# Second half of Q with the blocks of x in other buffers, and the first scores ahead of V's first quarter

## The reference, cut to what matters

```
h = layernorm(x)
q = rope(h @ Wq)    32 heads of 128;  k = rope(ctx @ Wk), v = ctx @ Wv    8 heads of 128
w = softmax(where(mask, 30 * tanh(q.k * scale / 30), -1e30))
x = x + (w @ v) @ Wo
x = x + base(layernorm(x)) + lora(layernorm(x))     top-2 of 8 experts, rank 16
```

## Time and profile before

| | us |
|---|---|
| median of 3 runs (lowest, highest) | 2150.79 (2147.84, 2157.55) |
| profiled execution, its own time | 2149.18 |
| its span in the trace | 2147.4 |
| TensorE busy in the span | 2129.3 (99%) |
| DVE, ACT, POOL busy | 1663.9, 882.2, 292.8 |

### The profile page before, as it was taken

The page is one execution under the profiler, slowest core; times in us unless marked ns, Lnnn a source line. Parts: engine busy times, 40 slices in busy tenths (PEclk is TensorE's granted clock), DMA queues, the critical chain, the costliest instruction groups (busy, mean ns, idle before and its releaser), DMA issues.

```text
span 2147.4 us, 26381 instructions
## 1 busy us (share of the span) xinstructions
PE 2129.3 (99%) x9429; PEld 1727.0 (80%) x9429; DVE 1663.9 (77%) x2571; ACT 882.2 (41%) x1342; POOL 292.8 (14%) x359
## 2 busy tenths in 40 slices
PE   9999999999999999998999999999999999999999
PEld 7888888888888888876778777777787777888887
DVE  6966889888887666676878789997998889857443
ACT  3323243222241111155555566655665556423221
POOL 0340001111131000013111111111112111100000
PEclk9999999999999999999999999999999999999999
DMA  8698597655596655698766786689677965696741
GB/s 327 233 343 285 212 336 275 230 212 216 215 338 230 212 202 200 235 272 271 198 197 187 225 242 181 205 271 276 193 194 218 306 187 161 212 373 263 293 183 64
DMA packets 201715, 508.50 MB, mean 237 GB/s; under 512 B 20592, under 2 KB 45808, under 8 KB 199536
## 3 DMA queue, kind: packets, MB, share of 16 engines
q1 hardware_dynamic: 181104, 443.31, 62.7%
q0 software_dynamic: 20480, 63.50, 9.3%
HBM read 357.26 MB, written 149.16 MB: 236 GB/s over the span
## 4 chain that ended last, share of the span: by engine, by line
PE 86%; DMA 7%; DVE 4%; issue 1%; ACT 1%; POOL 0%; SPq 0%; ACTq 0%; DVEq 0%; POOLq 0%
PE ps L377 28%; PE ps L379 28%; PE ps L378 28%; DMA X2D<-stg 2%; DMA RB<-rD 2%; DMA rD<-r 1%; PE ps L914 1%; DVE Rl L330 1%; DVE Y L984 1%; DMA raw<-gran 1%; DVE ps L330 1%; DMA r<-rT 1%; DVE Pl L330 0%; DVE ps L899 0%; DVE Al L330 0%
## 5 line engine op out<-in xcount | busy, mean ns | idle before, releaser
L377 PE MATMUL ps<-Ah,Rh 128*128 128x512 f32 x1024 | 399.6, 390 | 2.6 <-DVE Y L984 2.6
L379 PE MATMUL ps<-Ah,Rl 128*128 128x512 f32 x1024 | 399.2, 390 | 0.0
L378 PE MATMUL ps<-Al,Rh 128*128 128x512 f32 x1024 | 399.0, 390 | 0.0
L378 PE MATMUL ps<-Xq,qW 128*128 128x512 f32 x896 | 348.5, 389 | 0.0
L377 PE MATMUL ps<-Xq,qW 128*128 128x512 f32 x896 | 348.5, 389 | 0.0
L379 PE MATMUL ps<-Xq,qW 128*128 128x512 f32 x896 | 348.5, 389 | 0.0
L330 DVE TENSOR_TENSOR Rl<-raw,Rh 128x1024 fp32r<-128x1024 f32 x174 | 212.3, 1220 | 57.1 <-ACT Rh L326 56.7
L326 ACT ACTIVATE Rh<-raw 128x1024 fp32r<-128x1024 f32 x176 | 185.4, 1055 | 148.5 <-PE ps L379 118.0
L377 PEld LDWEIGHTS ps<-Ah,Rh 128*128 128x128 f32 x1024 | 192.5, 188 | 45.0 <-DVE Y L984 3.0
L379 PEld LDWEIGHTS ps<-Ah,Rl 128*128 128x128 f32 x1024 | 192.5, 188 | 40.5
L378 PEld LDWEIGHTS ps<-Al,Rh 128*128 128x128 f32 x1024 | 192.5, 188 | 40.1
(11 more groups left out here) (217 smaller groups left out, 3869.1 us busy)
## 6 DMA issues: line engine op xcount, KB each, us to landing
raw<-gran SPq DMA_DIRECT2D x177, 512.0 KB, 6.1
QSD<-qW SPq DMA_DIRECT2D x64, 512.0 KB, 3.0
qD<-qt SPq DMA_DIRECT2D x128, 256.0 KB, 3.2
qW<-QSD SPq DMA_DIRECT2D x64, 512.0 KB, 3.7
qf<-qD SPq DMA_DIRECT2D x64, 512.0 KB, 8.3
RB<-rD POOLq DMA_DIRECT2D x128, 256.0 KB, 7.0
qraw<-gran SPq DMA_DIRECT2D x48, 512.0 KB, 4.3
kD<-kst SPq DMA_DIRECT2D x32, 512.0 KB, 3.8
```

The costliest lines, as they stand in the source:

```text
L377: put("pe", waits, lambda e: e.matmul(pe_out, lh, rh, start=first, stop=False, skip_group_check=more))
L378: put("pe", [], lambda e: e.matmul(pe_out, lh, rl, start=False, stop=False, skip_group_check=more))
L379: return put("pe", [], lambda e: e.matmul(pe_out, ll, rh, start=False, stop=last, skip_group_check=more), mark)
```

## The change

In the second half of Q the blocks of x lie in other buffers. Product i reads block i as before, but from buffer Xq[ORDER[cp][i]]: 3, 2, 4, 0, 1, 5, 6 for products 0 to 6. The loads of the second half are listed in that order too. `late_q`, which lets the filler's first raw loads start, is still the first product of quad 13. In the plan, the scores of group 0 stand at t = -16, -15, -14, -13, so that TensorE's order is S0, VQ1, S1, S2, VQ2, S3, VQ3 where it was VQ1, S0, S1, VQ2, S2, S3, VQ3 (S0 to S3 are the four scores of group 0). Nothing else is changed; the number of instructions and of bytes is the same.

```diff
+        ORDER = [range(7), (3, 2, 4, 0, 1, 5, 6)]
+
         def x_load(cp):
             got = []
-            for n in range(7):
-                d = [dma(f(Xq[n][:, 2 * k:2 * k + 2, 1, :]), XcD[cp, n, :, 2 * k:2 * k + 2],
-                         x_free[n] + Xc_store[cp, n], f"d_xq{n}{k}", 512) for k in range(2)]
+            for i, n in enumerate(ORDER[cp]):
+                d = [dma(f(Xq[n][:, 2 * k:2 * k + 2, 1, :]), XcD[cp, i, :, 2 * k:2 * k + 2],
+                         x_free[n] + Xc_store[cp, i], f"d_xq{n}{k}", 512) for k in range(2)]
...
             def product(i, dst, first, waits):
                 s, wm, kept = next(weights)
+                x = ORDER[cp][i]
...
-                    m = three(dst, lh, ll, Xq[i][:, k, 0, :], Xq[i][:, k, 1, :], first and k == 0, k == 3,
+                    m = three(dst, lh, ll, Xq[x][:, k, 0, :], Xq[x][:, k, 1, :], first and k == 0, k == 3,
...
-                x_free[i] = [m]
+                x_free[x] = [m]
...
-                    late_q = x_free[0]
+                    late_q = x_free[ORDER[1][0]]
...
-        first = {0: ((-15, -14, -13, -12), -11, -9, (-7, -6, -5, -4)),
+        first = {0: ((-16, -15, -14, -13), -11, -9, (-7, -6, -5, -4)),
```

## The result

| | before | after |
|---|---|---|
| median, us (20 runs of each) | 2157.64 | 2164.14 |
| lowest and highest, us | 2138.53, 2167.76 | 2156.34, 2172.57 |
| profiled execution, us (span) | 2149.18 (2147.4) | 2156.43 (2154.6) |
| last matmul of Q to first of the projection, us | 64.5 | 77.3 |
| last matmul of Q to the one of the projection that waits for Y, us | 78.1 | 90.4 |

The ratio of the times is 1.0042, with a 95% interval of 1.0024 to 1.0060. It is worked out from all forty runs and is not the ratio of the medians, which lie 6.5 us apart; the means lie 9.2 us apart. The change makes the kernel slower, by 9 us (5 to 13), less than the 0.5% that I called no change, though the interval reaches past it. The forecast was 1 us faster.

What follows compares the result with a forecast made beforehand. TensorE bounds the kernel, busy 2129.3 of 2147.4 us; only its waits and half clock can be won. Terms of -0.8, zeros and -0.2 made -1.0 us, from 2150.8 to 2149.8; range 2144.5 to 2157.

Steps and rivals of the forecast that it cites:

- Later context: Context splits and V's weight loads after Q come later: cost 0, other bound a 5.4 us stall and 1.4 us half clock.
- The end of Q on the queues: Last store of Q 2 to 4 us earlier, as 2 MB load ahead of the rush; up to 3.7 us, counted at nothing.
- S0 in front: At Q's end S0 starts without a wait ahead of VQ1 and covers the wait for bank l0: 0.8 us gained.
- The start of the second half: Xq[3] and Xq[4], needed earlier from 627.7 on, fit narrowly: cost 0, bounds 0 and 3 us.
- The sum: Whole kernel: -0.8 for l0, three zeros, -0.2 for relief of the blocked exponential; together -1.0 us.
- B: Rival: raw ring late in the first filler quarters, VQ2 waits, ACT and DVE stand behind it: +4 us, 2154.8; chance 0.22.
- A: Rival: after Q, last store lands before 957, V7 split in time, DMA chain ends earlier: -5.5 us, 2145.3; chance 0.18.
- C: Rival: the start of the second half stalls for Xq[3] or Xq[4]: +2 us, 2152.8; chance 0.11.
- D: Rival: all stalls between Q's end and the attention go: 2140.1 us; chance 0.02.

Runs made afterwards that it cites:

- e3: Kernel before, with only the first split of the context for V also waiting for product 4 of the last quad (8.2 us late): ratio 1.0075.
- e15: Kernel before with the context late as in e3, plus eight extra raw buffers for V1, V2, V3, ctx3 and V4 to V7: ratio 1.0003.
- e9: Changed kernel with eight raw buffers of their own for the loads of V1, V2, V3, ctx3 and V4 to V7: ratio 1.0032.
- e2: Kernel before with only the scores of group 0 at their new places, old order of the buffers: ratio 1.0033.
- e1: Kernel before with only the new ORDER of the buffers, scores at their old places: ratio 1.0081.
- e7: Kernel before with the raw loads of V0, V1 and V2 put ahead of all context parts: ratio 0.9999.

## Why the prediction was wrong

**The failed step is "Later context": priced at 0, it costs 16 us (11 to 21) when it comes alone.** I saw its mechanism. V1's load moves by 8 us, V4 to V7 and ctx3 hang on the same ring, and the prediction says so. Then I priced it only at TensorE's next user of that data: VQ2 needs V1 at 939.6. There it was right. V1 was issued at 931.15, 1.8 us later than I had it (3.2 counted from Q's end, which came 1.3 us earlier), and landed in 3.4 us:

```profile
raw<-gran SPq DMA_DIRECT2D x1, 512.0 KB, 3.4
...
qD<-qt SPq DMA_DIRECT2D x1, 256.0 KB, 15.0
```

No wait at VQ2. But "V4, V5 and V7 come 4 to 5 us later by the same count" was where the price lay. They were issued 5 to 8 us later and landed 8 to 15 us later, and it was left unpriced, because the next check was V5's data on TensorE at 961. The users that matter stand on ACT and DVE, in fixed places ahead of the exponential of S3 and ahead of the reciprocal, and what waits for the chain behind them is the product at 988. e3 and e15 settle it for the late context on the kernel before: alone 1.0075, the same with the loads freed 1.0003. For the changed kernel the same waits are in the trace, but freeing its loads gave only 1.0032 for 1.0050 (e9), so how much of its own 9 us goes through the ring is not shown.

**"The end of Q on the queues" had the sign wrong, for the same reason.** I took the 2 MB loaded early as relief for what follows. But the DMA engines had been full before (shares of 1.01 and 1.05 from 928 to 936), and in after they had 4 us with nothing to do. What was moved ahead of the crowd was outweighed by what was pushed into it: from 916 to 948 they moved 7.4 MB, and 8.6 MB in before. The last store of Q was issued at 952.50, not 2 to 4 us earlier but 2.8 later, and took 15.0 us where it took 13.4. "The chain starts when VQ3 ends, 0.8 us earlier": it started 2.7 us later, since the row sums waited for the exponential.

**"S0 in front" was half right.** S0 follows Q at once (930.57, 930.80), kT was issued at 915.09, the table load hid. But qf, issued at 917.73 behind kT and vT, took 8.4 us for its first half and over 9 for the second, and not 7. It was split only from 928.24, and ACT idled 12.96 us for it. In the last 2.9 us of that the context could have been split, and V1's load was issued late for it. Bank l0 was read out at 936.4 and not at 935.5, though Q ended 1.3 us earlier than in the sum, since the low halves of q and of the context stood ahead of the rotation on the DVE, from 928.90 on. So the wait for bank l0 stayed at 0.73 us (was 0.66): the 0.8 us never came. And the step had a cost that I did not look for: alone, the early scores lose 0.33% (e2), in part by the wait of 2.85 us for kT, which the new order loads early, and in part by the reciprocal's new place in the DVE's queue. How large the share of the scores is in the change itself stays open, since the parts do not add (0.81 and 0.33 against 0.50%) and e9, which freed the loads, has a new wait of its own.

**"The start of the second half" was right.** TensorE has no wait where Xq[3] and Xq[4] are needed early:

```profile
627.00:650.00 23.00, 23.00 (x104) 19.03 (x103) 21.14 (x31) 8.34 (x16) 14.50 (x10) 1.00 0.83 295
```

**The sum.** It had -0.8, 0, 0, 0 and -0.2. Measured are +9 us (5 to 13). In the profiles the seam is 12.9 us longer, and 12.4 us with the wait for Y. The waits up to there are 0.73 + 2.75 + 3.89 + 6.82 + 1.47 + 2.08 = 17.7 us, and 0.66 + 2.46 + 2.23 + 2.59 = 7.9 in before: 9.8 more. The rest, 2.5 us, is of the size of the lower clock behind them: the mean clock from 930 to 1030 is 0.93, and was 0.97. The profiled executions differ by 7.25 us and not by 12.9. Of the 5.6 us between, 1.3 lie ahead of the seam (Q ends at 930.57 and 931.91) and 1.9 in waits behind it (2.6 + 2.0 us in before, 2.1 + 0.6 in after); the rest is not traced.

**The rivals.** B, the raw ring that runs late, was the nearest, at +4 us and a chance of 0.22. It named the ring and the fixed order of ACT and DVE, and put the wait at VQ2, for V1; its condition (a landing of over 7.5 us there) did not come true, and the loss came all the same by its second half, "when V5 or V7 is late". Its price was short by its own terms: 2 + 1.2 us and as much again are 6.4 us, not 4. A named the same wait, that in front of the fourth product with V, with the opposite sign. C and D did not happen. For A I had cited the Trainium skill (DMA: Bandwidth & Descriptors, Queues, rings and completion order): a DMA's semaphore lands only after every earlier write of the same DMA engine. The trace is in keeping with it, at 3.4 us for 512 KB into empty queues and 15.0 us for 256 KB in the crowd, though no run here parts it from a mere sharing of the engines; the inference that the crowd would be smaller was mine. The Trainium skill's figures (DMA: Bandwidth & Descriptors, Anatomy of one DMA), which it gives for the GpSimd path, had led to an estimate of 3.2 us for 512 KB. I had set it aside for the rows at 5.3 to 7.1; at 3.4 us measured, it was the nearer one at that place.

**The range** was too narrow at the top even for a right mechanism: B at twice its price is 2158.8 and the range ended at 2157, and the forecast rests on three runs of before whose median lay 7 us below that of all twenty.

## What to carry to other kernels

When a consumer behind a ring of buffers is delayed, don't price the consumer alone, price the loads: count the ring's depth, and ask whether the DMA engines fall idle while every buffer is full, and into what crowd those loads then go. In queues of a fixed order the price shows up at whatever stands behind a late load's user, so check every due item on each engine (here an exponential and a reciprocal of 0.25 us), not only TensorE's next use of the data. And measure such a change as the distance between two matmuls around it, beside the median, with the second one behind the last wait that it can move (here the wait for Y).

## What the runs showed of the hardware

The time of a DMA went by what was in flight. 512 KB took 3.4 us at 931, when the DMA engines had been idle, and 7.1 us at 922.9. The three loads of 512 KB issued at 941.87, 947.01 and 948.72 took 11.6, 15.6 and 17.2 us, with the DMA engines busy for 0.95 and 1.06 of the time from 940 to 948. A 256 KB store took 15.0 us at 952.5, and 8 KB took 7.7 us (r, issued at 957.06).

The stretches in which TensorE waited more were granted less clock. Mean granted clock from 930 to 1030: 0.97 in before, 0.93 in after, 0.90 in e3, at 92.06, 82.23 and 77.34 us of busy TensorE. The rows of e3 and of e15, in which all is as in e3 but the ring:

```profile
930.00:1030.00 100.00, 77.34 (x312) 57.91 (x311) 55.74 (x77) 48.34 (x78) 27.28 (x33) 0.90 0.85 237
```

```profile
930.00:1030.00 100.00, 89.81 (x383) 69.81 (x382) 72.13 (x105) 62.04 (x97) 25.03 (x35) 0.95 0.94 270
```

The same kernel, before, ran from 2138.53 to 2167.76 us in twenty runs, 1.4%. Part of it sits in waits of TensorE for exponentials between 1100 and 1900, where the kernels don't differ in their work: from 0 us (e1) to 6.6 us (e7), by no rule that I could find. Half clock came behind some of them: behind the 3.82 us at 1270 in e7 starts lie 0.42 us apart, behind the two of 1.0 us in before (1498.35 and 1700.37) they stay at 0.23. With that scatter an effect of 0.2% can't be told by the 6 to 12 runs that each experiment had.
